# Moving four of the sixteen S products of a deformable convolution from GpSimd to VectorE

## The chip, the core and the metric

The kernel runs on one core of one Trainium2 chip. The metric is the device time of one execution in microseconds (us), as the median over runs. Five engines of the core work on their own instruction streams and meet only at semaphores: TensorE (PE in the profile, its weight loads PEld), VectorE (DVE), ScalarE (ACT), GpSimd (POOL) and SyncE (SP), which starts most of the DMAs.

## The reference

The input `x` is 8 images of 64 channels and 16 by 16 pixels. Two residual stages follow each other:

```python
x = x + deformable_conv(group_norm(x), w_off, b_off, w_conv)
x = x + similarity_attention(group_norm(x), W, b)
```

The deformable convolution first computes, with a 3x3 convolution, 27 numbers for each pixel: a vertical and a horizontal offset and a mask for each of 9 taps. For each tap the normalised image is sampled at the shifted place by bilinear interpolation (zero outside the image) and multiplied by the sigmoid of the mask, and a 64 by 576 matrix maps the 9 x 64 samples to 64 channels. The second stage forms `relu(cosine similarity)**2` between all 256 pixels of an image and applies that 256 by 256 matrix to a linear map of the channels plus a bias.

## The kernel before, in words

The 8 images are worked on as 4 pairs (`PAIRS`); two images of 64 channels fill the 128 partitions. All data is float32.

**Sampling as a matrix.** Bilinear weights are a product of two hats, max(0, 1 - distance), one for the row and one for the column. With pixels on the partitions, `hats` holds for each pixel and tap the hat of each of 8 rows (`ROWS`) and each of 16 columns. `S` is their outer product: for a pixel and tap, one weight for each of 8 x 16 = 128 pixels of the window around it. A pair has 4 tiles of pixels (`TILES`: two halves of the image by two images), so S of a pair consists of 4 pieces, and each piece is one instruction of 128 x 1152 elements (9 taps x 128). All four pairs have 16 pieces. PE then transposes S in blocks of 128 x 128 (`turn`), ACT and a few times DVE copy the transposed blocks out of PSUM (`groups_out`), and PE multiplies the transposed S with the transposed image (`sample`).

**Who made which piece before.** Tiles 0, 2 and 3 are multiplied by DVE (`multiply` in the vector block, L833); tile 1 (`POOL_TILE`) is multiplied by POOL (`multiply` in the gpsimd block, L310). Before that POOL multiplies the row hats by the sigmoid mask (`mask_rows`, L316), and both multiplies wait for it. POOL also computes the powers of the variances (`power`, L303) and squares the similarities of pairs 0 to 2 (`square`, L324, two instructions for a pair). Later work waits for two semaphores, `S_dve` and `S_pool`.

**Groups cross tiles.** PE transposes S in 9 groups of 4 blocks for a pair. 9 taps a tile is no multiple of 4, so the third group of tile 0 (blocks 8 to 11) holds blocks of tile 1 as well. `turn(k, 0)` therefore waits at its third group for S of tile 1, which `wait_S` in `turn` expresses.

**Order of work.** Each engine's order is written out by hand. The loop over k runs one pair ahead: while pair k is sampled, offsets and hats of pair k+1 are prepared, and attention of pair k-1 is done. The parts near the change are:

- DVE, before the loop: distances and hats of pair 0's half 0 (L800, L812, L814), distances of half 1, `multiply(0, 0)`, hats of half 1 (L812, L814), shift (L772), `normalise(0, 1)` (L785, writes `gpad` for the convolution of pair 1), `multiply(0, 2)`.
- DVE, in loop step k: hats of pair k+1, `scale_t(k-1)` (L881, L883, L889), `multiply(k+1, 0)`, `normalise(0, k+2)`, `multiply(k+1, 2)`, then `scale_attended(k-1)`, `finish(k-1)` and `residual(k)`; `multiply(k, 3)` comes early in the step.
- POOL, in loop step k: `power`, `mask_rows(k+1)`, `multiply(k+1, 1)`, `square(k-1)`.
- PE, at the end of loop step k: `similarities(k-1)`, `sample(k, 3)`, `turn_t(k-1)`, `turn(k+1, 0)`, `attend(k-1)` (L513, waits for the squares of POOL), `project(k)` (L444). The next step begins with `convolve(k+2)` (L383) and `turn(k+1, 1)`.

S has two buffers (pairs alternate). A second version of the same code (`general`) stands in the program for offsets that reach further than the window; it isn't run on these inputs.

Of the kernel before, what the change touches and what calls it, by code (L numbers as in the profile page):

```python
# [30 lines left out]
ALU = mybir.AluOpType  # L31
# [8 lines left out]
TILES = 4  # L40
# [25 lines left out]
def run_pairs(nc, general, far, y_sb, stored, x, w_off, b_off, w_conv, w1, b1, consts, out):  # L66
# [7 lines left out]
    SLOTS = TILES * TAPS * BLOCKS  # L74
    GROUPS = SLOTS // GROUP
    S_BUFS = 1 if general else 2
    POOL_TILE = 1
    DVE_GROUPS = (1, 4, 7, 10, 13, 16) if general else (6,)

    way = "general_" if general else ""  # L80
# [1 line left out]
    with ctx:  # L82
# [3 lines left out]
        def sem(name):  # L86
            return ctx.enter_context(nc.semaphore(way + name))
# [74 lines left out]
        dist_ready, mask_ready, abs_ready, hats_ready, hy_masked = (  # L162
            sem("dist_ready"), sem("mask_ready"), sem("abs_ready"), sem("hats_ready"), sem("hy_masked"))
        xT_done, xT_out = sem("xT_done"), sem("xT_out")
        S_dve, S_pool = sem("S_dve"), sem("S_pool")
        ring_full, ring_act, ring_dve = sem("ring_full"), sem("ring_act"), sem("ring_dve")
        samp_done, samp_out = sem("samp_done"), sem("samp_out")
        out_done, x1_ready = sem("out_done"), sem("x1_ready")
# [34 lines left out]
        def last_group(tile):  # L203

            return ((tile + 1) * TAPS * BLOCKS - 1) // GROUP
# [7 lines left out]
        index = {item: i for i, item in enumerate(items)}  # L213
# [13 lines left out]
                if emptied_by(is_dve, i):  # L227
                    eng.wait_ge(s, emptied_by(is_dve, i))

        def S_count(k, tile, on_pool):  # L230

            return sum(1 for n in range(TILES * k + tile + 1) if (n % TILES == POOL_TILE) == on_pool)

        def wait_S(eng, k, tile):
            on_pool = tile == POOL_TILE
            eng.wait_ge(S_pool if on_pool else S_dve, S_count(k, tile, on_pool))

        def hats_of(k, j):

# [5 lines left out]
        def hats_count(k, j):  # L245

            return j + 1 if k == 0 else k + 2

        def S_part(k, tile):

            hy, hx = hats_of(k, tile // 2)
            s, of_s = slice(TAPS * (tile % 2), TAPS * (tile % 2) + TAPS), slice(TAPS * tile, TAPS * tile + TAPS)
            return (S[:, k % S_BUFS, of_s, :].rearrange("p s (r c) -> p s r c", c=W),
                    hy[:, s, :].unsqueeze(3).to_broadcast([128, TAPS, ROWS, W]),
                    hx[:, s, :].unsqueeze(2).to_broadcast([128, TAPS, ROWS, W]))
# [33 lines left out]
        @block.gpsimd  # L289
        def _(pool):  # L290
            nc.gpsimd.memset(boff_col[:], 0.0).then_inc(zeroed, 1)
            nc.gpsimd.memset(warm[:], 0.0).then_inc(zeroed, 1)
            nc.gpsimd.memset(woff_T[:], 0.0).then_inc(zeroed, 1)
            nc.gpsimd.memset(gpad[:], 0.0).then_inc(zeroed, 1)
            nc.gpsimd.memset(grows[:], 0.0).then_inc(zeroed, 1)
            nc.gpsimd.memset(w1_T[:], 0.0).then_inc(zeroed, 1)

            def power(part):
                i, n, lo, hi = part
                pool.wait_ge(gn_var[i], n + 1)  # L300
                if part == GN1_FIRST:
                    pool.wait_ge(table_in, 16)
                nc.gpsimd.tensor_tensor(rstd[:, i, lo:hi], var[:, i, lo:hi], minus_half[:, lo:hi], ALU.pow).then_inc(gn_rstd[i], 1)  # L303

            def multiply(k, tile):
                pool.wait_ge(hy_masked, hats_count(k, tile // 2))
                if k >= S_BUFS:
                    pool.wait_ge(ring_full, index["turn", k - S_BUFS, last_group(tile)] + 1)
                o, a, b = S_part(k, tile)
                nc.gpsimd.tensor_tensor(o, a, b, ALU.mult).then_inc(S_pool, 1)  # L310

            def mask_rows(k, js):
                pool.wait_ge(hats_ready, hats_count(k, js[-1]))
                hy = hats[:, k % 2, js[0]:js[-1] + 1, 0:2 * TAPS * ROWS].rearrange("p j (s r) -> p j s r", r=ROWS)
                m = mask[:, k % 2, 2 * js[0]:2 * js[-1] + 2].rearrange("p (j t) s -> p j (t s)", t=2)
                nc.gpsimd.tensor_tensor(hy, hy, m.unsqueeze(3).to_broadcast([128, len(js), 2 * TAPS, ROWS]),  # L316
                                        ALU.mult).then_inc(hy_masked, 1)

            def square(k):
                for b in range(2):  # L320
                    wait_emptied(pool, index["sim", k, b])
                    if k >= 1:
                        pool.wait_ge(att_done, k)
                    nc.gpsimd.tensor_tensor(sim2[:, b], sim[:, b], sim[:, b], ALU.mult).then_inc(sim2_ready, 1)  # L324

            power(GN1_FIRST)
            power(GN1_REST)
            mask_rows(0, (0,))
            multiply(0, POOL_TILE)
            mask_rows(0, (1,))  # L330
            for k in range(PAIRS + 1):
                if k >= 1:
                    power(gn2(k - 1))
                if k + 1 < PAIRS:
                    mask_rows(k + 1, (0, 1))
                    multiply(k + 1, POOL_TILE)
                if 1 <= k < PAIRS:
                    square(k - 1)

# [395 lines left out]
        def _(dve):  # L735
# [51 lines left out]
            def distances(k, j):  # L787

                if j == 0:
                    dve.wait_ge(mask_ready, k + 1)  # L790
                if k == 0 and j == 0:
                    dve.wait_ge(table_rest_in, 16)
                if k >= 2:
                    dve.wait_ge(S_pool, S_count(k - 2, TILES - 1, True))
                    dve.wait_ge(S_dve, S_count(k - 2, TILES - 1, False))
                offs = prep_ps[:, 128:256].rearrange("p (t o) -> p t o", o=OFFC)
                ty, tx = (h.rearrange("p (t s) r -> p t s r", s=TAPS) for h in hats_of(k, j))
                rows = cy[:, j, :] if general else cy_window
                for n, (t, of, size) in enumerate(((ty, rows, ROWS), (tx, cx, W))):
                    nc.vector.tensor_tensor(t, offs[:, 2 * j:2 * j + 2, TAPS * n:TAPS * n + TAPS].unsqueeze(3).to_broadcast([128, 2, TAPS, size]),  # L800
                                            of.unsqueeze(1).unsqueeze(1).to_broadcast([128, 2, TAPS, size]),
                                            ALU.add).then_inc(dist_ready, 1)
                if j == 1 and not general:
                    nc.vector.tensor_reduce(reach[:, k:k + 1], offs[:, :, 0:TAPS], AX.XY, ALU.max,
                                            apply_absolute_value=True).then_inc(reach_own, 1)
# [110 lines left out]
            make_hats(0, (0,))  # L916
            distances(0, 1)
            multiply(0, 0)
            make_hats(0, (1,))
            scale_and_shift(GN1_REST)  # L920
            normalise(0, 1)
# [2 lines left out]
            for k in range(PAIRS + 1):  # L924
                main, after = k < PAIRS, k >= 1
                ahead = k + 1 < PAIRS
                if k == PAIRS - 1 and not general:
                    farthest()
                if after:
                    statistics(1, k - 1)  # L930
                if main:
                    groups_out(k, 1)
                    multiply(k, 3)
                if k == PAIRS:
                    scale_attended(k - 2)
                if after:
                    group_variance(gn2(k - 1))
                if k == PAIRS:
                    finish(k - 2)
                if after:  # L940
                    scale_and_shift(gn2(k - 1))
                    normalise(1, k - 1)
                if main:
                    groups_out(k, 2)
                if ahead:
                    distances(k + 1, 0)
                    distances(k + 1, 1)
                    make_hats(k + 1, (0, 1))
                if main:
                    groups_out(k, 3)  # L950
                if k == PAIRS:
                    scale_t_last()
                elif after:
                    scale_t(k - 1)
                if ahead:
                    multiply(k + 1, 0)
                if k + 2 < PAIRS:
                    normalise(0, k + 2)
                if k == PAIRS - 1 and not general:
                    set_far()  # L960
                if k == PAIRS:
                    square_last()
                if ahead:
                    multiply(k + 1, 2)
                    groups_out(k + 1, 0)
                if after and k != PAIRS - 1:
                    scale_attended(k - 1)
                    finish(k - 1)
                if main:
                    residual(k)  # L970
# [29 lines left out]
```

## Time and profile before

| quantity | value |
|---|---|
| median of 3 runs | 104.29 us (104.21, 104.29, 104.40) |
| span of the profiled execution | 102.7 us |
| mean granted TensorE clock, share of full speed | 0.980 |
| busy: PE, PEld, DVE, ACT, POOL | 88.0, 62.9, 63.1, 43.5, 28.4 us |
| DVE pieces of S (L833) | 12 instructions, 18.1 us |
| POOL pieces of S (L310) | 4 instructions, 11.0 us |

The span is from the first to the last instruction of the profiled execution. The time of that same execution is not given separately; the runs lie 1.5 to 1.7 us above its span. A busy share is an average over the whole span, so it doesn't say which engine sets the pace of a stage; the rows below are read for that.

### The profile page before, as it was taken

To read this page: it belongs to the slowest core of one execution; us is meant where nothing else is said; L and a number is where in the kernel's file an instruction comes from. 1 tells how busy PE (TensorE), PEld (TensorE's weight loads), DVE (VectorE), ACT (ScalarE), POOL (GpSimd) and SP (SyncE) were. 2 spreads that over 40 slices of the span, in tenths; PEclk is the share of its full clock that TensorE was granted. 3 is DMA by queue.
4 is the path that set the end of the run, shared out by engine and by line. 5 is a ranking of instruction groups with operands and counts; after the bars stand their busy time and mean duration, and the time that the engine had idled before them with its cause. 6 is when DMAs were issued, how large, how long until landed. Compare 5 with 4: busy or idle time off the path is not lost.

```text
span 102.7 us, 1892 instructions
## 1 busy us (share of the span) xinstructions
PE 88.0 (86%) x705; PEld 62.9 (61%) x705; DVE 63.1 (61%) x136; ACT 43.5 (42%) x88; POOL 28.4 (28%) x31
## 2 busy tenths in 40 slices
PE   5999994579998699999989999993999998999600
PEld 4655973368675388766668876662677655675200
DVE  1334239994388936699994669993396470738400
ACT  3203022645578605664940566494056573015100
POOL 7020016910019400209830020987002025020000
PEclk9999999999999999999999999999999999999975
DMA  2840000000000000000001000000000000010020
GB/s 49 248 121 16 10 0 0 0 6 0 0 3 0 6 0 0 0 0 6 3 0 51 0 6 0 0 0 0 32 19 6 0 0 0 0 51 0 0 67 0
DMA packets 2906, 1.80 MB, mean 18 GB/s; under 512 B 1561, under 2 KB 2841, under 8 KB 2895
## 3 DMA queue, kind: packets, MB, share of 16 engines
q1 hardware_dynamic: 2271, 1.36, 4.5%
q10 hardware_dynamic: 624, 0.31, 1.1%
q8 instruction: 6, 0.10, 0.5%
q14 instruction: 5, 0.04, 0.1%
HBM read 1.14 MB, written 0.52 MB: 16 GB/s over the span
## 4 chain that ended last, share of the span: by engine, by line
PE 48%; issue 22%; POOL 12%; DVE 9%; ACT 2%; POOLq 1%; ACTq 0%
PE prep_ps L383 9%; PE ring L414 9%; POOL sim L324 8%; PE samp_ps L433 8%; PE out_ps L346 6%; PE out_ps L444 4%; DVE hats L812 3%; PE att_ps L352 2%; PE att_ps L513 2%; POOL S L310 2%; PE ring L501 1%; DVE S L833 1%; DVE hats L800 1%; POOL rstd L303 1%; PE ring L491 1%
## 5 line engine op out<-in xcount | busy, mean ns | idle before, releaser
L414 PE MATMUL ring<-table,S 128*128 128x128 f32 x144 | 19.6, 279 | 2.2 <-issue 1.9
L650 ACT COPY ST<-ring 128x512 f32<-128x512 f32 x32 | 17.5, 595 | 8.1 <-PE ring L414 7.9
L414 PEld LDWEIGHTS ring<-table,S 128*128 128x128 f32 x144 | 15.5, 141 | 7.4 <-issue 6.0
L433 PE MATMUL samp_ps<-ST,xT 128*64 128x320 f32 (+1 forms) x128 | 19.1, 418 | 0.3 <-ACT sampled L659 0.3
L833 DVE TENSOR_TENSOR S<-hats 128x1152 f32<-128x1152 f32 x12 | 18.1, 1523 | 0.8 <-POOL hats L316 0.8
L659 ACT COPY sampled<-samp_ps 128x640 f32<-128x640 f32 x16 | 11.1, 692 | 9.2 <-PE samp_ps L433 9.1
L303 POOL TENSOR_TENSOR rstd<-var,table 128x1 f32<-128x1 f32 (+1 forms) x6 | 3.7, 622 | 36.2 <-DVE var L766 36.2
L433 PEld LDWEIGHTS samp_ps<-ST,xT 128*64 128x64 f32 x128 | 9.9, 136 | 5.5 <-issue 3.0
L310 POOL TENSOR_TENSOR S<-hats 128x1152 f32<-128x1152 f32 x4 | 11.0, 2743 | 0.3
L383 PE MATMUL prep_ps<-gpad,woff_T 128*64 128x128 f32 x144 | 10.1, 302 | 0.6 <-DVE gpad L785 0.6
L383 PEld LDWEIGHTS prep_ps<-gpad,woff_T 128*64 128x64 f32 x144 | 9.5, 155 | 1.5 <-DVE gpad L785 0.9
L324 POOL TENSOR_TENSOR sim<-sim 128x512 f32<-128x512 f32 x6 | 8.6, 1448 | 6.6 <-ACT sim L679 6.6
L444 PE MATMUL out_ps<-sampled,wconv_T 128*64 128x256 f32 x80 | 9.5, 382 | 0.4 <-ACT sampled L659 0.4
L346 PE MATMUL out_ps<-warm_w 128*128 128x256 bf16 (+1 forms) x39 | 8.6, 350 | 1.1 <-DVE warm_w L736 1.1
L316 POOL TENSOR_TENSOR hats<-hats,mask 128x288 f32<-128x288 f32 (+1 forms) x5 | 2.9, 586 | 18.5 <-DVE hats L814 18.5
L444 PEld LDWEIGHTS out_ps<-sampled,wconv_T 128*64 128x64 f32 x80 | 6.2, 137 | 2.8 <-ACT sampled L659 0.7
L618 ACT ACTIVATE conv_sb<-prep_ps,boff_col 128x128 f32<-128x128 f32 x4 | 1.5, 368 | 14.4 <-PE prep_ps L383 14.4
L848 DVE TENSOR_TENSOR x_sb<-out_ps,x_sb 128x256 f32<-128x256 f32 x4 | 1.7, 424 | 7.8 <-PE out_ps L444 7.8
L346 PEld LDWEIGHTS out_ps<-warm_w 128*128 128x128 bf16 x39 | 4.6, 126 | 2.7 <-DVE warm_w L736 1.1
L513 PE MATMUL att_ps<-sim,tT 128*64 128x256 f32 x32 | 4.3, 386 | 2.1 <-POOL sim L324 2.1
L883 DVE RECIPROCAL inv_norm<-norm 128x256 f32<-128x256 f32 x3 | 5.3, 1753 | 0.1
L800 DVE TENSOR_TENSOR hats<-prep_ps,table 128x144 f32<-128x144 f32 (+1 forms) x16 | 5.1, 373 | 0.1
(94 smaller groups left out, 98.4 us busy)
## 6 DMA issues: line engine op xcount, KB each, us to landing
x_sb<-x SPq DMA_DIRECT2D x4, 128.0 KB, 2.8
out<-y_sb SPq DMA_DIRECT2D x4, 128.0 KB, 1.7
table<-consts ACTq DMA_DIRECT2D x1, 130.0 KB, 3.1
woff_nat<-w_off SPq DMA_DIRECT2D x1, 121.5 KB
table<-consts ACTq DMA_DIRECT2D x1, 92.0 KB, 3.7
wconv_nat<-w_conv ACTq DMA_DIRECT2D x1, 80.0 KB, 4.2
wconv_nat<-w_conv SPq DMA_DIRECT2D x1, 80.0 KB, 2.6
boff_col<-b_off SPq DMA_DIRECT2D x4, 0.1 KB
```

The costliest lines, as they stand in the source:

```text
L310: nc.gpsimd.tensor_tensor(o, a, b, ALU.mult).then_inc(S_pool, 1)
L324: nc.gpsimd.tensor_tensor(sim2[:, b], sim[:, b], sim[:, b], ALU.mult).then_inc(sim2_ready, 1)
L346: pe.matmul(ps, warm_w[:, 0:128], warm_w[:, 0:ps.shape[1]], start=True, stop=True)
L383: mm = pe.matmul(prep_ps[64 * j:64 * j + 64, 0:HALF], woff_T[:, t, :], gpad[:, k % 2, r:r + 8, c:c + W], start=(t == 0), stop=(t == TAPS - 1))
L414: mm = pe.transpose(ring[i % RING][:, 128 * n:128 * n + 128], S[:, k % S_BUFS, s, 128 * w:128 * w + 128], ident)
L433: mm = pe.matmul(samp_ps[64 * h:64 * h + 64, a, 64 * lo:64 * hi], xT[:, k % 2, w if general else 2 * j + a, C * b:C * b + C], ST[:, k % 2, ...
L444: mm = pe.matmul(out_ps[64 * b:64 * b + 64, 0:N], wconv_T[:, t, :], sampled[:, k % 2, b, t, :], start=(t == 0), stop=(t == LOW - 1))
L513: mm = pe.matmul(att_ps[64 * b:64 * b + 64, N:2 * N], tT[:, m, 64 * b:64 * b + 64], sim2[:, b, m, :], start=(m == 0), stop=(m == 1))
L650: nc.scalar.copy(dst, ring[i % RING][:]).then_inc(ring_act, 1)
L659: nc.scalar.copy(dst, src).then_inc(samp_out, 1)
L800: nc.vector.tensor_tensor(t, offs[:, 2 * j:2 * j + 2, TAPS * n:TAPS * n + TAPS].unsqueeze(3).to_broadcast([128, 2, TAPS, size]), of.unsque ...
L833: nc.vector.tensor_tensor(o, a, b, ALU.mult).then_inc(S_dve, 1)
```

## The change

VectorE makes tile 1 of each pair too, right behind tile 0 in its order, and GpSimd makes none. The semaphore `S_pool` goes away; `S_dve` counts all four pieces of a pair, in the order 0, 1, 2, 3.

```diff
-    POOL_TILE = 1
...
-        S_dve, S_pool = sem("S_dve"), sem("S_pool")
+        S_dve = sem("S_dve")
...
-        def S_count(k, tile, on_pool):
-
-            return sum(1 for n in range(TILES * k + tile + 1) if (n % TILES == POOL_TILE) == on_pool)
-
         def wait_S(eng, k, tile):
-            on_pool = tile == POOL_TILE
-            eng.wait_ge(S_pool if on_pool else S_dve, S_count(k, tile, on_pool))
+            eng.wait_ge(S_dve, TILES * k + tile + 1)
...
-            def multiply(k, tile):
-                pool.wait_ge(hy_masked, hats_count(k, tile // 2))
-                if k >= S_BUFS:
-                    pool.wait_ge(ring_full, index["turn", k - S_BUFS, last_group(tile)] + 1)
-                o, a, b = S_part(k, tile)
-                nc.gpsimd.tensor_tensor(o, a, b, ALU.mult).then_inc(S_pool, 1)
-
...
             mask_rows(0, (0,))
-            multiply(0, POOL_TILE)
             mask_rows(0, (1,))
             for k in range(PAIRS + 1):
...
                 if k + 1 < PAIRS:
                     mask_rows(k + 1, (0, 1))
-                    multiply(k + 1, POOL_TILE)
...
                 if k >= 2:
-                    dve.wait_ge(S_pool, S_count(k - 2, TILES - 1, True))
-                    dve.wait_ge(S_dve, S_count(k - 2, TILES - 1, False))
+                    dve.wait_ge(S_dve, TILES * (k - 1))
...
             distances(0, 1)
             multiply(0, 0)
+            multiply(0, 1)
             make_hats(0, (1,))
...
                 if ahead:
                     multiply(k + 1, 0)
+                    multiply(k + 1, 1)
                 if k + 2 < PAIRS:
                     normalise(0, k + 2)
```

## Rows read from the trace of the kernel before

**Rows 1.** First line of the page.
```profile
span 102.7 us, 1892 instructions
```

**Rows 2.** Busy time of each engine by stretch: a PE stretch, two round attention.
```profile
core 0: us, PE busy (x) PEld busy (x) DVE busy (x) ACT busy (x) POOL busy (x), PEclk, DMA share, GB/s
...
35.20:50.20 15.00, 14.98 (x134) 10.75 (x133) 11.38 (x24) 7.99 (x17) 4.18 (x4) 1.00 0.01 1
50.20:53.40 3.20, 2.67 (x23) 2.24 (x25) 3.15 (x3) 2.41 (x6) 1.92 (x2) 1.00 0.01 3
...
68.20:72.20 4.00, 2.42 (x21) 2.04 (x23) 2.06 (x1) 2.16 (x5) 2.96 (x2) 1.00 0.00 0
```

**Rows 3.** PE in time order: start, length, line, idle before and releaser.
```profile
20.54 0.63 PE L414 MATMUL ring<-table,S 128*128 128x128 f32 x4 [0.96 <-issue]
21.82 2.19 PE L383 MATMUL prep_ps<-gpad,woff_T 128*64 128x128 f32 x36 [0.65 <-DVE gpad L785]
...
34.61 0.63 PE L414 MATMUL ring<-table,S 128*128 128x128 f32 x4 [0.95 <-issue]
...
52.27 1.08 PE L513 MATMUL att_ps<-sim,tT 128*64 128x256 f32 x8 [0.51 <-POOL sim L324]
...
71.30 1.08 PE L513 MATMUL att_ps<-sim,tT 128*64 128x256 f32 x8 [1.58 <-POOL sim L324]
```

**Rows 4.** VectorE in time order, hats and S of pairs 0 and 1.
```profile
15.68 0.39 DVE L812 TENSOR_SCALAR hats<-hats 128x432 int32<-128x432 int32 x1
...
17.09 1.35 DVE L833 TENSOR_TENSOR S<-hats 128x1152 f32<-128x1152 f32 x1
18.35 2.33 DVE L812 TENSOR_SCALAR hats<-hats 128x432 int32<-128x432 int32 x1
...
21.21 0.55 DVE L785 TENSOR_SCALAR gpad<-x_sb,rstd,shift 128x256 f32<-128x256 f32 x1
21.68 2.61 DVE L833 TENSOR_TENSOR S<-hats 128x1152 f32<-128x1152 f32 x2
...
31.15 1.36 DVE L833 TENSOR_TENSOR S<-hats 128x1152 f32<-128x1152 f32 x1 [0.80 <-POOL hats L316]
32.42 2.24 DVE L785 TENSOR_SCALAR gpad<-x_sb,rstd,shift 128x256 f32<-128x256 f32 x1
```

**Rows 5.** GpSimd in time order: its four pieces of S, the last squares.
```profile
17.08 3.36 POOL L310 TENSOR_TENSOR S<-hats 128x1152 f32<-128x1152 f32 x1
...
31.19 3.32 POOL L310 TENSOR_TENSOR S<-hats 128x1152 f32<-128x1152 f32 x1
...
46.81 2.15 POOL L310 TENSOR_TENSOR S<-hats 128x1152 f32<-128x1152 f32 x1
...
64.78 2.15 POOL L310 TENSOR_TENSOR S<-hats 128x1152 f32<-128x1152 f32 x1
...
84.04 2.04 POOL L324 TENSOR_TENSOR sim<-sim 128x512 f32<-128x512 f32 x2 [5.75 <-ACT sim L679]
```

**Rows 6.** VectorE and GpSimd in short windows from 48.5 to 53.4 us, pair 2.
```profile
48.60 1.57 DVE L833 TENSOR_TENSOR S<-hats 128x1152 f32<-128x1152 f32 x1
...
49.40 1.68 POOL L324 TENSOR_TENSOR sim<-sim 128x512 f32<-128x512 f32 x1 [0.44 <-ACT sim L679]
...
50.09 1.12 DVE L785 TENSOR_SCALAR gpad<-x_sb,rstd,shift 128x256 f32<-128x256 f32 x1
...
51.03 1.09 POOL L324 TENSOR_TENSOR sim<-sim 128x512 f32<-128x512 f32 x1
51.14 2.19 DVE L833 TENSOR_TENSOR S<-hats 128x1152 f32<-128x1152 f32 x1
```

**Rows 7.** VectorE and GpSimd in short windows from 66.5 to 71.2 us, pair 3.
```profile
66.57 1.58 DVE L833 TENSOR_TENSOR S<-hats 128x1152 f32<-128x1152 f32 x1
...
67.36 1.69 POOL L324 TENSOR_TENSOR sim<-sim 128x512 f32<-128x512 f32 x1 [0.42 <-ACT sim L679]
...
68.07 2.19 DVE L833 TENSOR_TENSOR S<-hats 128x1152 f32<-128x1152 f32 x1
...
69.01 2.15 POOL L324 TENSOR_TENSOR sim<-sim 128x512 f32<-128x512 f32 x1
```

## Prediction, made before the changed kernel was run

> **What bounds the kernel now.** I read the page first: the span is 102.7 us [rows 1], and the runs lie 1.5 to 1.7 us above it, so a change of the span is carried one to one onto the median of 104.29. Then I cut PE's work into stretches. In the long ones, such as 35.2 to 50.2 us, PE is busy for 14.98 of 15.00 us at full granted clock [rows 2]: between its waits PE sets the pace, and the other engines follow it. So only a wait of PE that gets shorter or longer can move the end. PE in time order shows the waits that concern S, five of them [rows 3]:
>
> - 20.54, third group of `turn(0, 0)`, idle 0.96, and right behind it 21.82, `convolve(1)`, idle 0.65 behind DVE's `gpad`. PE takes them in order, and the second decides: it would start at 21.82 wherever the group before it stood.
> - 34.61, third group of `turn(1, 0)`, idle 0.95. The view says "issue" (no releaser found), but the code makes the group wait for S of tile 1, and POOL's piece ends at 31.19 + 3.32 = 34.51 [rows 5], 0.10 before.
> - 52.27 and 71.30, `attend(0)` and `attend(1)`, idle 0.51 and 1.58 behind POOL's squares.
>
> Last I put DVE and POOL side by side, to see what they do to each other.
>
> **DVE and POOL take turns.** In pair 0 a DVE and a POOL piece start together. DVE's takes 17.09 + 1.35 = 18.44; POOL's takes 3.36, though the same instruction takes 2.15 at 46.81; DVE's L812, 0.39 at 15.68, takes 2.33 [rows 4, 5]. In pair 3 the ends are 68.15 (DVE), 69.05 (POOL), 70.26 (DVE), 71.16 (POOL), each instruction having been issued before the one ahead of it had ended [rows 7]. So one waits for the whole instruction of the other, and when both want to go, they alternate. What one costs once it is let go:
>
> - a DVE piece behind a POOL instruction: 46.81 + 2.15 = 48.96 to 50.17, 66.93 to 68.15, 69.05 to 70.26: 1.21 to 1.22 [rows 5 to 7]; alone 1.35, and two back to back 2.61, so the second adds 1.26 [rows 4];
> - a square behind a DVE piece: 50.17 to 51.08, 68.15 to 69.05, 70.26 to 71.16: 0.90 [rows 6, 7]; two alone take 2.04 [rows 5];
> - a POOL piece behind a DVE piece: 18.44 to 20.44, 32.51 to 34.51: 2.00 [rows 4, 5];
> - `normalise` behind a POOL instruction: 34.51 to 34.66, 51.08 to 51.21: 0.13 to 0.15 [rows 4 to 6].
>
> RECIPROCAL and the other instructions of `scale_t` run on DVE while POOL makes its pieces of pairs 2 and 3, and those two pieces stay at their short 2.15.
>
> **The change part by part.** Removed are POOL's four pieces, added are four on DVE. I go through the pairs; times are on the old clock, each with the shift before it taken out.
>
> *Pair 0.* DVE's second piece follows at once and ends at 17.09 + 2.61 = 19.70. L812 is issued 0.09 before that, as it was at 18.35, runs freely for 0.39 and ends at 20.00, where it ended at 20.68 [rows 4]. Everything behind it on DVE (L814, L772, L785, which feeds `convolve(1)`) moves with it. PE's third group is ready at 19.80 instead of 20.54 and done well before `convolve(1)`. Gain 0.68. It would be lost if something else held `convolve(1)`; its weights and bank have been ready since the first convolution, so I find none.
>
> *Pair 1.* Two DVE pieces from 31.15 end at 33.76; POOL's ended at 34.51 [rows 4, 5]. PE's group moves from 34.61 to 33.86, while the work ahead of it ends 0.95 before 34.61, at 33.66 [rows 3], and so doesn't take the place of the wait. Gain 0.75. `normalise(0, 2)` isn't held by POOL any more, and `multiply(1, 2)` ends earlier too.
>
> *Pair 2.* POOL's piece was hidden before: it ended at 48.96, cost DVE's first piece 0.22, and PE didn't wait for it. Now DVE's first piece ends at 48.60 + 1.34 = 49.94. The squares were issued at 49.40, released by ACT and not by POOL's own queue (idle 0.44 before them), so they don't move up [rows 6]. By turns: square 1 to 50.84, the new piece to 52.05, square 2 to 52.95, `normalise` to 53.08, `multiply(2, 2)` to some 54.4. Square 2 ended at 52.12. `turn(2, 0)`, ahead of `attend(0)` in PE's order, gets its third group at 52.15 and takes 0.63, to 52.78, so the square still decides. **Loss 0.83.** Queued behind the new piece on DVE are `normalise(0, 3)`, needed by `convolve(3)` only after `attend(0)` and `project(1)`, and `scale_attended(0)`, which waits for the same late `attend(0)`: neither sets a new wait.
>
> *Pair 3.* Here is no `normalise` in between. First piece to 66.57 + 1.34 = 67.91, square 1 to 68.81, new piece to 70.02, square 2 to 70.92, third piece to 72.13. Square 2 ended at 71.16 [rows 7]. PE's third group runs 70.12 to 70.75, still ahead of it. Gain 0.24, because POOL's piece no longer holds up DVE's first. The third piece ends 1.87 later than before, when `attend(1)` ends too (71.06 + 1.08); DVE's `scale_attended(1)` needs both, and PE wants the piece only after `project(2)`.
>
> The semaphore waits themselves I cost at nothing: DVE's waits for `ring_full` and for older pieces are long met, and a wait less is queued on POOL.
>
> Sum: -0.68 - 0.75 + 0.83 - 0.24 = **-0.84 us**; span 102.7 to 101.9, median 104.29 to 103.45, say 103.5.
>
> Bounds: a second piece in a row costs 1.26 or, at most, the 1.35 of a lone one, which takes 0.09 from each of the first two gains. In pair 2 the loss lies between 0 (if another engine than POOL held `attend`) and 1.1 (each of the three hand-overs 0.1 dearer, where the rows scatter by 0.01). Pair 3 lies between 0 and -0.24.
>
> A rule of the Trainium skill says otherwise on the second piece. "VectorE: DVE Perf Modes", section "The DRAIN you can't avoid", states that the next instruction does not start until the pipe of the one before is empty; by that the two gains would be 0.59 and 0.66 and the sum -0.66, 103.6 us. The trace disagrees, if a little: 2.61 for two against 2 x 1.35.
>
> **The rivals.**
>
> *A, slower: no turns.* If a free place goes to the engine that just had it, three DVE pieces stand in a row ahead of the squares. Pair 3: 67.91 + 2 x 1.26 = 70.43, squares to 71.33 and 72.35, 1.19 late. Pair 2: 49.94 + 1.26 + 0.13 + 1.26 = 52.59, squares to 53.49 and 54.51, 2.39 late. With the gains of pairs 0 and 1 that is -1.43 + 3.58 = +2.15, 106.4 us. It decides as soon as the two `attend`s together come over 1.43 late. For it speaks that DVE has three pieces queued as never before; against it, that square 1 got in between two queued DVE pieces at 68.15 [rows 7]. If POOL keeps its place instead, the squares are early but the new piece is late (51.87 + 1.21 = 53.08 in pair 2, after which PE's group holds `attend(0)` to about 53.8): some +0.5, 104.8; 69.05 to 70.26 speaks against it.
> The Trainium skill, "SBUF — State Buffer", section "SBUF: two separate sides", calls the port pair that the two engines share an exclusive lock held for a whole instruction, against a DVE instruction with two SBUF inputs. The rows show just that; the page does not say who is next when both wait, which is what A turns on.
>
> *B, much faster: squares and pieces don't hold each other up*, the long ones being long for another reason. Then pair 2 has its new piece at 51.2 and `attend(0)` at 51.9 (-0.35), pair 3 its group to 69.9 and `attend(1)` then (-1.4): -3.2, 101.1 us. Four hand-overs that agree to 0.01 speak against it.
>
> *C, about the same: one of the first two gains doesn't reach PE*, because another wait stands right behind the one removed: -0.84 + 0.68 = -0.16 or -0.84 + 0.75 = -0.09, 104.1 to 104.2 us. PE's next work in both places has what it needs, as far as I can see.
>
> *D: PE's two idle pieces before `attend(0)` lower its clock.* Before, an idle of 1.58 at 71.30 left the granted clock at 1.00 [rows 2, 3]; I price it with the slower side.
>
> **How the numbers follow.** Forecast 0.76, with its own range 103.2 to 103.8 from the bounds; A 0.09; B 0.04; C 0.07; D and what I don't see 0.04. A measurement can tell 0.2%, 0.21 us, from no change. Faster: forecast, B and some of C, 0.82; same: most of C, 0.06; slower: A and D, 0.12. The range takes in the forecast's and C's near edge: 103.0 to 104.1.
>
> **What would show it.** After: DVE pieces at 17.1 in a pair of 2.6, L812 back to 0.4, `convolve(1)` at 21.15; the third group of pair 1 within 0.3 us behind the one before it. In the stretch of pair 2 two DVE pieces with a square between them, and `attend(0)` held 0.8 longer; in pair 3 three pieces and two squares that alternate. Wrong would be: squares behind all the pieces (A), pieces of 1.35 beside squares of 1.0 (B), or a PE wait in pair 0 or 1 with a new releaser (C).

## The result and the profile after

| | before | changed |
|---|---|---|
| median of 4 runs | 104.31 us (104.21 to 104.40) | 103.14 us (102.25 to 104.51) |
| span of the profiled execution | 102.7 us | 100.9 us |
| busy DVE, POOL | 63.1, 28.4 us | 64.6, 18.0 us |

The ratio is 0.9857 with a 95% interval of 0.9814 to 0.9901. Ratios, here and below, leave out the runs that lie more than 1.5% above the shortest run of their kernel, which is the run of 104.51 us here, and later 14 of 23 runs of before beside 2 of 12 of the changed kernel, which brings those two closer together than their medians are. So 102.25, 102.92 and 103.36 are compared with the runs before. The change made the kernel faster in this comparison, as forecast, but by 1.4% where 0.8% was forecast, and the median of those three, 102.92, lies just below the stated range of 103.0 to 104.1; the median of all four, 103.14, lies just inside it.

In the chain of waits and in time order the middle of the kernel looks as drawn up. PE of the changed kernel in time order, the rows that answer to [rows 3], and the two third groups that now wait:

```profile
19.41 0.63 PE L399 MATMUL ring<-table,S 128*128 128x128 f32 x4 [0.22 <-DVE S L817]
20.74 2.19 PE L368 MATMUL prep_ps<-gpad,woff_T 128*64 128x128 f32 x36 [0.70 <-DVE gpad L770]
...
32.80 0.63 PE L399 MATMUL ring<-table,S 128*128 128x128 f32 x4 [0.22 <-DVE S L817]
...
50.35 0.63 PE L399 MATMUL ring<-table,S 128*128 128x128 f32 x4 [1.07 <-DVE S L817]
51.30 1.08 PE L498 MATMUL att_ps<-sim,tT 128*64 128x256 f32 x8 [0.32 <-POOL sim L311]
...
69.16 0.63 PE L399 MATMUL ring<-table,S 128*128 128x128 f32 x4 [1.07 <-DVE S L817]
70.10 1.08 PE L498 MATMUL att_ps<-sim,tT 128*64 128x256 f32 x8 [0.31 <-POOL sim L311]
```

The waits of 0.96 and 0.95 us for POOL's piece are down to 0.22, and now have a releaser by name. In pairs 2 and 3 there is a new wait of 1.07 us for the piece that moved to DVE, but the squares still end last ahead of both `attend`s.

DVE of the changed kernel in time order, against [rows 4]:

```profile
16.70 2.61 DVE L817 TENSOR_TENSOR S<-hats 128x1152 f32<-128x1152 f32 x2
19.23 0.37 DVE L796 TENSOR_SCALAR hats<-hats 128x432 int32<-128x432 int32 x1
...
30.07 2.63 DVE L817 TENSOR_TENSOR S<-hats 128x1152 f32<-128x1152 f32 x2 [0.80 <-POOL hats L303]
32.61 0.41 DVE L770 TENSOR_SCALAR gpad<-x_sb,rstd,shift 128x256 f32<-128x256 f32 x1
```

Two pieces in a row take 2.61 and 2.63. The `hats` instruction is back from 2.33 to 0.37 and `normalise` from 2.24 to 0.41, because POOL has nothing running there.

DVE and POOL of the changed kernel in short windows from 46.8 to 52.6 us, pair 2, against [rows 6]:

```profile
46.79 1.35 DVE L817 TENSOR_TENSOR S<-hats 128x1152 f32<-128x1152 f32 x1
...
47.58 1.46 POOL L311 TENSOR_TENSOR sim<-sim 128x512 f32<-128x512 f32 x1 [2.66 <-ACT sim L664]
...
48.06 2.19 DVE L817 TENSOR_TENSOR S<-hats 128x1152 f32<-128x1152 f32 x1
...
49.00 2.15 POOL L311 TENSOR_TENSOR sim<-sim 128x512 f32<-128x512 f32 x1
...
50.18 1.12 DVE L770 TENSOR_SCALAR gpad<-x_sb,rstd,shift 128x256 f32<-128x256 f32 x1
...
51.22 1.34 DVE L817 TENSOR_TENSOR S<-hats 128x1152 f32<-128x1152 f32 x1
```

and from 65.6 to 71.2 us, pair 3, against [rows 7]:

```profile
65.60 1.35 DVE L817 TENSOR_TENSOR S<-hats 128x1152 f32<-128x1152 f32 x1
66.39 1.46 POOL L311 TENSOR_TENSOR sim<-sim 128x512 f32<-128x512 f32 x1 [2.66 <-ACT sim L664]
66.86 2.19 DVE L817 TENSOR_TENSOR S<-hats 128x1152 f32<-128x1152 f32 x1
...
67.81 2.15 POOL L311 TENSOR_TENSOR sim<-sim 128x512 f32<-128x512 f32 x1
...
68.98 2.19 DVE L817 TENSOR_TENSOR S<-hats 128x1152 f32<-128x1152 f32 x1
```

The ends in pair 3, each a start plus its length, read 66.95 (DVE), 67.85 (POOL), 69.05 (DVE), 69.96 (POOL), 71.17 (DVE): strictly by turns, 0.90 or 0.91 for a square and 1.20 or 1.21 for a piece, as in the kernel before.

**Where 1.8 us of span went.** I cut both spans in three: a head up to the first `hats` instruction of DVE, which nothing of the change precedes; a middle from there to the end of DVE's last instruction; and a tail in which no compute instruction runs, only the last output's DMA and the end of the program. The ends are these rows, of the kernel before

```profile
14.97 0.67 DVE L800 TENSOR_TENSOR hats<-prep_ps,table 128x144 f32<-128x144 f32 x2
...
97.01 0.42 DVE L902 TENSOR_TENSOR y_sb<-y_sb,x_sb 128x256 f32<-128x256 f32 x1
```

and of the changed one

```profile
14.59 0.67 DVE L784 TENSOR_TENSOR hats<-prep_ps,table 128x144 f32<-128x144 f32 x2
...
95.80 0.42 DVE L886 TENSOR_TENSOR y_sb<-y_sb,x_sb 128x256 f32<-128x256 f32 x1
```

The middle went from 97.43 - 14.97 = 82.46 to 96.22 - 14.59 = 81.63: 0.83 less, where the prediction's sum is 0.84. The head gave another 0.38 and the tail (102.7 - 97.43 = 5.27 to 100.9 - 96.22 = 4.68) another 0.59. Whether head and tail belong to the change is the question of the first experiments.

### The profile page after: what moved, and what is told of

It reads as the page before. It is cut to its first block, busy times and chain, and to the rows that moved or that the text cites. A ratio compares the mean times of both kernels' runs of the same rounds, so it can differ in the third digit from the quotient of the medians.

```text
span 100.9 us, 1890 instructions
## 1 busy us (share of the span) xinstructions
PE 87.6 (87%) x705; PEld 62.3 (62%) x705; DVE 64.6 (64%) x140; ACT 43.6 (43%) x88; POOL 18.0 (18%) x27
## 3 DMA queue, kind: packets, MB, share of 16 engines
q1 hardware_dynamic: 2271, 1.36, 4.7%
HBM read 1.14 MB, written 0.52 MB: 16 GB/s over the span
## 4 chain that ended last, share of the span: by engine, by line
PE 40%; issue 24%; DVE 14%; POOL 12%; DMA 3%; ACT 2%; POOLq 1%; ACTq 0%
PE prep_ps L368 9%; POOL sim L311 9%; PE ring L399 7%; DVE S L817 5%; PE out_ps L429 4%; PE samp_ps L418 4%; PE out_ps L331 3%; DMA x_sb<-x 3%; DVE hats L784 2%; PE att_ps L337 2%; PE att_ps L498 2%; DVE hats L798 1%; POOL hats L303 1%; PE ring L486 1%; DVE hats L796 1%
## 5 line engine op out<-in xcount | busy, mean ns | idle before, releaser
L817 DVE TENSOR_TENSOR S<-hats 128x1152 f32<-128x1152 f32 x16 | 23.6, 1504 | 0.8 <-POOL hats L303 0.8
L311 POOL TENSOR_TENSOR sim<-sim 128x512 f32<-128x512 f32 x6 | 9.2, 1548 | 11.1 <-ACT sim L664 11.1
L368 PEld LDWEIGHTS prep_ps<-gpad,woff_T 128*64 128x64 f32 x144 | 9.0, 149 | 1.6 <-DVE gpad L770 0.9
L828 DVE COPY ST<-ring 128x512 f32<-128x512 f32 x4 | 2.8, 689 | 3.4 <-PE ring L399 3.4
```

Of the source, the lines that this page charges most:

```text
L368: mm = pe.matmul(prep_ps[64 * j:64 * j + 64, 0:HALF], woff_T[:, t, :], gpad[:, k % 2, r:r + 8, c:c + W], start=(t == 0), stop=(t == TAPS - 1))
L817: nc.vector.tensor_tensor(o, a, b, ALU.mult).then_inc(S_dve, 1)
```

## Experiments

The theory T: the change moves only the middle, by the four terms of the sum; head and tail vary from run to run by themselves. The rival R: they are part of the change. Beside that each of the four terms is tried alone, and the turn-taking is taken away.

**The two kernels again.** No edit; each was run under two more labels.

> The changed kernel once more, unaltered. Theory T (the change moves only the middle; the head before the hats of pair 0 and the tail after the last VectorE instruction vary from run to run by themselves): the middle, from the first L784 to the end of the last L886, is 81.63 us again within 0.05, while the convolution of pair 0 (3.13 us in the first profile) and the tail (4.7 us) may come out differently, and the times spread over more than 1 us. Rival R (a shorter head and tail belong to the changed program): convolution 3.1, tail 4.7 again, and the time at 102.3 to 103.4.

> The kernel before once more, unaltered. T: the middle (first L800 to the end of the last L902) is 82.46 us again within 0.05; the first convolution (3.60) and the tail (5.27) may differ from the first profile. R: 3.6 and 5.3 again, always longer than in the changed kernel.

> The changed kernel a third time, for the parts outside the middle. T: middle 81.64 again; head and tail anywhere in the spread seen so far (first hats at 13.5 to 15.0 us, tail 4.7 to 6.6). R: first hats no later than 14.6 and tail no longer than 4.8.

> The kernel before a third time, for the parts outside the middle. T: middle 82.47 again; first hats anywhere from 13.3 to 15.2 us, tail anywhere from 4.7 to 6.6.

| profiled execution | time | span | head | first convolution | middle | tail |
|---|---|---|---|---|---|---|
| before, first profile | not given | 102.7 | 14.97 | 3.65 | 82.46 | 5.27 |
| before, second | 103.22 | 101.5 | 13.63 | 3.14 | 82.47 | 5.40 |
| before, third | 105.19 | 103.5 | 14.32 | 3.15 | 82.46 | 6.72 |
| changed, first profile | 102.92 | 100.9 | 14.59 | 3.17 | 81.63 | 4.68 |
| changed, second | 101.98 | 100.1 | 13.62 | 3.11 | 81.66 | 4.82 |
| changed, third | 104.00 | 102.3 | 15.16 | 4.06 | 81.69 | 5.45 |

The longest head of the six is one of the changed kernel, and so R falls for the head. The tails of the changed kernel reach 5.45, those of before start at 5.27: they overlap, though the longest is one of before. R in its own words, a tail of 4.8 at most in the changed kernel, fell with 5.45; that a part of the tail hangs on the kernel isn't excluded by three of each. The two third profiles also went a little past the spread that was expected of them (head 15.16, tail 6.72). (Where the expectations give the first convolution as 3.60 and 3.13, that is its share of the chain of waits; the table has the length of its row.) The middle stays within 0.06 us in each kernel, and the difference of the two is 0.77 to 0.84 in every pairing. The third profile of the changed kernel is slower (104.00) than the second of before (103.22), although its middle is 0.78 shorter.

In the timed comparison the changed kernel had a median of 102.98 over 12 runs (101.98 to 105.04) beside 104.12 of before over 23 runs (102.30 to 106.04). The medians are 1.14 us apart, nearer to the 0.8 of the middle than to the 1.8 by which the first two spans differ; the ratio is 0.9944 with an interval from 0.9886 to 1.0001. The kernel before under its second label had 104.32 in the same comparison (12 runs, 102.64 to 106.30), ratio 1.0032 to itself with an interval from 0.9946 to 1.0119, so a difference of 0.8% is at the edge of what such a comparison can tell. The three runs of before that the prediction saw lay closer together (0.2 us) than this kernel's runs do.

What varies in the head is the speed of PE. In all twelve profiles of this document the first hats stand 1.06 or 1.07 us behind the end of the first convolution, so the head is the start of that convolution plus its length. Two profiles of the same program, the kernel before, in windows, first profile:

```profile
core 0: us, PE busy (x) PEld busy (x) DVE busy (x) ACT busy (x) POOL busy (x), PEclk, DMA share, GB/s
...
4.20:8.00 3.80, 3.70 (x18) 2.50 (x17) 1.12 (x6) 0.00 (x0) 0.55 (x1) 1.00 0.54 140
8.00:9.40 1.40, 1.40 (x8) 0.93 (x8) 0.43 (x2) 0.41 (x2) 0.00 (x0) 1.00 0.08 15
...
12.50:14.00 1.50, 1.50 (x20) 1.33 (x16) 0.00 (x0) 0.05 (x1) 0.00 (x0) 1.00 0.00 0
```

and second profile:

```profile
4.20:8.00 3.80, 3.80 (x21) 2.89 (x20) 1.11 (x6) 0.00 (x0) 0.55 (x1) 1.00 0.54 143
8.00:9.40 1.40, 1.40 (x7) 0.74 (x6) 1.23 (x4) 0.96 (x2) 0.00 (x0) 0.50 0.08 16
```

The same small matmuls get through in a different number between 4.2 and 8.0 us (18 and 21), though both stretches show a granted clock of 1.00, and in one execution the clock is then at half (the lower level, 1.2 of 2.4 GHz) for a while and in the other not. The first convolution, the same 36 matmuls, takes 3.65 us in the first profile and 3.14 in the second:

```profile
10.25 3.65 PE L383 MATMUL prep_ps<-gpad,woff_T 128*64 128x128 f32 x36
21.82 2.19 PE L383 MATMUL prep_ps<-gpad,woff_T 128*64 128x128 f32 x36 [0.65 <-DVE gpad L785]
```

```profile
9.43 3.14 PE L383 MATMUL prep_ps<-gpad,woff_T 128*64 128x128 f32 x36
20.47 2.19 PE L383 MATMUL prep_ps<-gpad,woff_T 128*64 128x128 f32 x36 [0.65 <-DVE gpad L785]
```

The steps between those small matmuls tell more. Two of them in the first profile of before,

```profile
5.18 0.29 PE L346 MATMUL out_ps<-warm_w 128*128 128x128 bf16 x1
...
5.64 0.29 PE L346 MATMUL out_ps<-warm_w 128*128 128x128 bf16 x1
```

in its second,

```profile
4.97 0.23 PE L346 MATMUL out_ps<-warm_w 128*128 128x128 bf16 x1
...
5.35 0.23 PE L346 MATMUL out_ps<-warm_w 128*128 128x128 bf16 x1
```

and in the kernel of the last experiment below, where the length changes on the way, with a window around that place:

```profile
7.12 0.23 PE L331 MATMUL out_ps<-warm_w 128*128 128x128 bf16 x1
...
7.52 0.29 PE L331 MATMUL out_ps<-warm_w 128*128 128x128 bf16 x1
```

```profile
7.00:8.00 1.00, 1.00 (x6) 0.67 (x7) 0.00 (x0) 0.00 (x0) 0.00 (x0) 0.64 0.05 1
```

The step is 0.46 us in the first profile and 0.38 in the second. Six of the twelve profiles have the longer step throughout, and heads of 14.32 to 15.31; the other six have the shorter one up to 7 us at least, and heads of 13.26 to 13.72. The first and third profiles of before and of the changed kernel are in the first group, the second of each in the other, so each kernel comes in both groups. In the six with the shorter step the record shows the clock falling to half between 7.3 and 8.4 us and rising again inside the first convolution, and that convolution takes 2.19 plus half of its time at half clock, to 0.05 us: in the second profile of before the mean clock of its 3.14 us is 0.68, which is 2.01 us at half, and 2.19 + 1.00 = 3.19. In the other six the record shows 1.00 all through the convolution, which still takes 3.15 to 4.06, so the clock on record doesn't account for them.

From the second convolution on (2.19 in all) the profiles of each kernel agree to 0.06 us. The longest middle of the changed kernel, 81.69, is that of its third profile, in which the granted clock is at half (0.50) from 18 to 20 us. What decides which group an execution falls into, and the length of its tail, was not tried and stays open.

**One pair at a time.** `POOL_PAIRS` names the pairs whose tile 1 stays on POOL; the rest of the edit follows from it.

```diff
     POOL_TILE = 1
+    POOL_PAIRS = (1, 2, 3)
...
+        def of_pool(k, tile):
+
+            return tile == POOL_TILE and k in POOL_PAIRS
...
                 if ahead:
                     multiply(k + 1, 0)
+                    if not of_pool(k + 1, POOL_TILE):
+                        multiply(k + 1, POOL_TILE)
```

> VectorE makes tile 1 of pair 0 alone. My steps: the convolution of pair 1 starts 0.68 us earlier behind the first hats (6.15 us instead of 6.85) and the whole middle is 0.68 shorter than before, 81.78 us. Rival C (another wait stands right behind the removed one): middle 82.4.

> VectorE makes tile 1 of pair 1 alone. My steps: from the convolution of pair 1 to the projection of pair 0 0.75 us less than before, middle 81.72 us. Rival C: middle 82.4.

> VectorE makes tile 1 of pair 2 alone. My steps: middle +0.83 us, 83.29 us, slower than before by 0.8%. Rival (squares and pieces don't hold each other up): middle 82.1 or less, not slower.

> VectorE makes tile 1 of pair 3 alone. My steps: two squares and three pieces alternate, second attend 0.24 us earlier, middle 82.22 us. Rival (three pieces queued keep the squares out): second attend about 1.2 us late, middle 83.6.

| DVE makes tile 1 of | middle | against 82.46 | my step | time, runs |
|---|---|---|---|---|
| pair 0 alone | 81.78 | -0.68 | -0.68 | 102.24, 1 |
| pair 1 alone | 81.71 | -0.75 | -0.75 | 103.78, 1 |
| pair 2 alone | 83.30 | +0.84 | +0.83 | 105.05, 6 |
| pair 3 alone | 82.23 | -0.23 | -0.24 | 105.19, 1 |

The four add up to -0.82, what the whole change does (-0.77 to -0.84). Pair 2 alone also shows in the time: ratio 1.0163 against before, interval 1.0092 to 1.0234, which is more than the 0.8% of its middle, while the medians over all runs (105.05 and 104.12) are 0.9% apart. The single times of the others say nothing: pair 3 alone, the better by 0.23 in its middle, has a tail of 6.56 and a time of 105.19.

PE of the kernel with pair 2 alone, the two `attend`s in time order:

```profile
51.63 1.08 PE L520 MATMUL att_ps<-sim,tT 128*64 128x256 f32 x8 [0.32 <-POOL sim L329]
...
70.67 1.08 PE L520 MATMUL att_ps<-sim,tT 128*64 128x256 f32 x8 [1.57 <-POOL sim L329]
```

With its first hats at 13.50 the first stands 38.13 us behind them, where the kernel before has 52.27 - 14.97 = 37.30: 0.83 later, and that delay is still there at the second (57.17 against 56.33). PE took none of it back.

**Pair 2 left on POOL.** `POOL_PAIRS = (2,)`, so that the three gains stay and the loss goes.

> VectorE makes tile 1 of pairs 0, 1 and 3; GpSimd keeps that of pair 2. My steps: -0.68 -0.75 +0 -0.24 = -1.67 us in the middle against before, that is 80.79 us, and 0.84 faster than the changed kernel. Rival (turn-taking is not what lengthens pair 2): no better than the changed kernel, middle 81.6.

The middle is 80.83, 1.63 less than before and 0.80 less than the changed kernel. The time is 102.28 (6 runs), ratio to before 0.9841, interval 0.9752 to 0.9930.

**No squares on POOL beside the pieces.** The changed kernel, with ScalarE squaring pairs 0 and 1:

```diff
-                if 1 <= k < PAIRS:
+                if k == PAIRS - 1:
                     square(k - 1)
...
                 elif after:
                     relu_similarities(k - 1)
-                if k + 2 < PAIRS:
-                    normalised_rows(k + 2)
+                if 1 <= k < PAIRS - 1:
+                    square(k - 1)
                 if main:
                     sampled_out(k, 3)
                 if after and k < PAIRS:
                     t_out(k - 1)
+                if k + 2 < PAIRS:
+                    normalised_rows(k + 2)
```

where `square` in the scalar block is `activation(sim2[:, b], sim[:, b], ACT.Square)` with the waits that POOL's had.

> The changed kernel with the squares of pairs 0 and 1 on ScalarE, right behind its two relus, and the normalised rows of pair k+2 moved behind the copy of t. If the squares and the S pieces lengthen each other, all pieces now take 1.26 to 1.36 us (2.6 for two in a row, 3.9 for three), the first attend starts about 1.1 us earlier than in the changed kernel and the second another 1.1, and the middle comes to 79.4 us, 3.1 less than before: time about 100.8. Rival (the pieces are long for another reason, or attend waits for something else): pieces of 1.6 to 2.2 us stay, middle 81 or more.

All instructions of the line that makes S, their lengths (shortest, median, longest) in this kernel:

```profile
L826 DVE TENSOR_TENSOR S<-hats x16: 1327/1348/1359, 15.4 to 70.6; 128x1152 f32<-128x1152 f32 x16
```

and DVE and PE in time order:

```profile
45.46 2.62 DVE L826 TENSOR_TENSOR S<-hats 128x1152 f32<-128x1152 f32 x2
...
63.03 3.88 DVE L826 TENSOR_TENSOR S<-hats 128x1152 f32<-128x1152 f32 x3
```

```profile
48.73 1.08 PE L498 MATMUL att_ps<-sim,tT 128*64 128x256 f32 x8
...
66.31 1.08 PE L498 MATMUL att_ps<-sim,tT 128*64 128x256 f32 x8
```

No piece is longer than 1.36 us, where the changed kernel has them up to 2.19, and no idle time is shown ahead of either `attend`. Counted from the first hats they start 1.24 and then another 1.22 us earlier than in the changed kernel (35.47 and 53.05 against 36.71 and 55.51). The middle is 79.17, 3.29 less than before and 0.2 better than expected; the time 100.65 (6 runs, 99.45 to 101.23), ratio to before 0.9743, interval 0.9683 to 0.9803. This version beats both kernels: its longest run is below the shortest of the changed one. That the squares on POOL lengthen the pieces is shown by it; that the pieces lengthen the squares (1.46 and 2.15 us in pairs 2 and 3, two in 2.04 where no piece is near), and that it goes by turns, by the rows of pairs 2 and 3. The edit also moves `normalised_rows` to a later place on ScalarE, which was not tried alone, so how much of the 2.46 us beyond the changed kernel comes from the squares is not separated.

## Why the prediction was wrong in its range, and right in its other steps

- *PE sets the pace between its waits; only its waits count.* Right. Each shift measured at one wait is found again, to 0.06 us, at the end of the middle.
- *Pair 0, -0.68.* Right: `convolve(1)` stands 6.15 us behind the first hats instead of 6.85, -0.70.
- *Pair 1, -0.75.* Right: `project(0)` goes from 20.20 behind the hats to 18.76, that is -0.74 on top.
- *Pair 2, +0.83.* Right: `attend(0)` goes from 37.30 to 36.71, so 0.85 of the 1.44 gained are given back. No other wait took the loss up.
- *Pair 3, -0.24.* Right: `attend(1)` goes from 56.33 to 55.51, another -0.23.
- *The second piece in a row costs 1.26.* Right (2.61 and 2.63, and 3.88 for three). The prediction set a rule of the Trainium skill beside it ("VectorE: DVE Perf Modes", section "The DRAIN you can't avoid"), by which it would be the full 1.35. It left out that the same section has a next instruction that is not held start earlier; the trace agrees with that.
- *The rivals.* A fell with the turns in pair 3, B with the pieces of 2.19, C with the waits of 0.22, with a `convolve(1)` that still waits for `gpad` alone, and with the kernels that move pair 0 or pair 1 alone (-0.68 and -0.75 in the middle). D did not come: the granted clock of the changed kernel is 1.00 from 46.0 to 53.0 us and from 64.0 to 72.0.
- **The step that failed** is the first one: "a change of the span is carried one to one onto the median of 104.29", together with "A measurement can tell 0.2%, 0.21 us, from no change". It puts the scatter of head, tail and of the distance from span to time at nothing. I took the scatter of the metric from three runs that lay within 0.2 us, and built the range from the middle alone. In further runs this same kernel took 102.30 to 106.30 us, and its time lay 1.62 to 2.06 us above the span of the same execution. In the twelve profiles, of eight kernels, the head was 13.26 to 15.31 us and the tail 4.68 to 6.72, while the middle repeats to 0.06. In the profiled pair, head and tail gave 0.38 + 0.59 = 0.97 us; the 0.38 is not the change's, and that any of the 0.59 is has not been shown. So the term of 0.84 had the right size (0.83), and the 1.4% of the first comparison holds about 0.5% of scatter by the account of the profiles. That three runs had their median 0.08 us below the range, and not inside it, was chance. The wider comparison, 0.6% with an interval that reaches from 1.1% to nothing, is consistent with 0.8% and can't confirm it alone; the middles do.
- *The range was also narrower than its own bounds.* Added up, the bounds of the terms give -1.67 to -0.15 us, that is 102.6 to 104.1, where the prediction went on with 103.2 to 103.8 and then 103.0 to 104.1. A range from 102.6 would have held 102.92, but by luck, since the scatter is not in it either.

## What to carry to other kernels

Two engines that hold each other up are best read by their ends: write the ends of both in one column and see who goes after whom, and the price of each hand-over comes out to a hundredth. Work taken off one of the two doesn't vanish: it pays where PE waited for it and the other engine's turn is free, and costs where a third instruction must now wait one turn more; so move it pair by pair, which gave 1.63 us here where moving all gave 0.83, or take the other party off the two engines as well, which with a reorder on ScalarE gave 3.29. And before giving a range of a few tenths, look for the parts of the span in which the profiled work does not set the time, the first microseconds and the last, and count them into the range even if the runs at hand lie close together.

## What the runs showed of the hardware that was not expected

- The 36 matmuls of the first convolution took between 2.82 and 4.06 us in twelve profiles, the same 36 of the second always 2.19. In six of the profiles the granted clock on record, at half for a part of that stretch, accounts for the length to 0.05 us; in the other six it is 1.00 throughout, as in the first profile of before, which took 3.65.
- The stretch after the last compute instruction took 4.68 to 6.72 us, with the same output DMA in it (median 1.7 us from issue to landing in the profiles of before and after).
- An instruction that has already waited for the other engine costs less than it does alone: a square ends 0.90 us behind a DVE piece (1.02 in an undisturbed row of two), a DVE piece 1.20 to 1.22 behind a square (1.35 alone). So a queue of alternating instructions costs 0.12 to 0.15 us for each less than the sum of its parts.
